# Joined stores and new instruction orders in a one-core vision transformer layer

## What is computed

```
p = img2patches(x)                                  # 1152 x 768
h = layernorm(layernorm(p) @ W + b)                 # patch embedding, 192 wide, in float32
h = h + attention(layernorm(h))                     # 12 heads of 16; cosine attention over the 32 images
                                                    #   at one patch position
h = h + bitlinear(silu(gate) * up)                  # up, gate = bitlinear(layernorm(h)); 192 -> 2 x 512 -> 192
```

## Time and profile before

| | |
|---|---|
| Median of three runs | 127.58 us |
| The profiled execution | 127.43 us, of which the span is 125.5 us |
| Busy, share of the span | PE 106.9 us (85%), DVE 102.5 (82%), ACT 86.1 (69%), POOL 70.9 (57%) |
| Chain that ended last, by engine | PE 33%, DVE 25%, POOL 18%, issue 9%, DMA 4%, ACT 3% |
| DMA | 7.77 MB; written 0.88 MB in 18 stores of 48 KB |

### The profile page before, as it was taken

How to read it: one execution, slowest core, us unless ns; L and a number is a source line. 1 busy time by engine, 2 the same in 40 slices (tenths; PEclk the granted TensorE clock), 3 DMA queues, 4 the chain that set the end, 5 groups by cost and what they waited for, 6 DMA issues and landing times.

```text
span 125.5 us, 4783 instructions
## 1 busy us (share of the span) xinstructions
PE 106.9 (85%) x1851; PEld 84.7 (67%) x1854; DVE 102.5 (82%) x384; ACT 86.1 (69%) x175; POOL 70.9 (57%) x164
## 2 busy tenths in 40 slices
PE   5998998999999998999999999899989976844500
PEld 5988898799787886976776766777567743423100
DVE  4039438999999999999999999999999999967200
ACT  0406537899998853296587995985999978996500
POOL 7002007349341096175269789998899898885000
PEclk9999999999999999999999999999999999999985
DMA  4999999969700000000000000000001010110110
GB/s 83 237 272 219 177 181 275 228 120 162 136 22 3 0 5 3 5 5 3 5 5 5 0 0 5 5 5 3 5 8 28 7 43 21 30 35 21 34 46 33
DMA packets 24095, 7.77 MB, mean 62 GB/s; under 512 B 20038, under 2 KB 23495, under 8 KB 24072
## 3 DMA queue, kind: packets, MB, share of 16 engines
q1 hardware_dynamic: 20838, 6.82, 27.0%
q10 hardware_dynamic: 3234, 0.64, 2.7%
HBM read 6.58 MB, written 0.88 MB: 59 GB/s over the span
## 4 chain that ended last, share of the span: by engine, by line
PE 33%; DVE 25%; POOL 18%; issue 9%; DMA 4%; ACT 3%; ACTq 2%; POOLq 0%; DVEq 0%
PE bank L662 7%; POOL yw L359 5%; DMA xs<-in_x_dram 4%; PE bank L667 3%; PE bank L684 3%; POOL r L367 3%; PE bank L685 3%; PE bank L646 3%; PE bank L713 2%; ACTq L242 2%; POOL yy L351 2%; DVE ss L913 2%; PE bank L701 2%; PE bank L584 2%; DVE mx L971 2%
## 5 line engine op out<-in xcount | busy, mean ns | idle before, releaser
L662 PE MATMUL bank<-w_emb_g,xT 128*128 128x192 f32 x72 | 13.5, 330 | 1.1 <-DVE h0s L879 1.0
L866 DVE BATCH_NORM_STATS2 bst<-xs 128x6 f32<-128x384 f32 x18 | 9.0, 540 | 6.0 <-DMA xs<-in_x_dram 6.0
L315 POOL TENSOR_TENSOR rs<-mv,mhalf 128x1 f32<-128x1 f32 x9 | 5.5, 609 | 14.6 <-DVE mv L888 14.6
L662 PEld LDWEIGHTS bank<-w_emb_g,xT 128*128 128x128 f32 x72 | 11.6, 190 | 2.2 <-issue 2.0
L461 ACT ACTIVATE xp<-xs,mv 128x768 f32<-128x768 f32 x9 | 8.4, 935 | 5.7 <-DVE mv L872 5.7
L577 PE MATMUL bank<-ident 128*128 128x128 f32 x60 | 8.8, 315 | 1.8 <-POOL ident L289 1.5
L359 POOL TENSOR_TENSOR yw<-yy,gout_bc 128x512 f32<-128x512 f32 x8 | 10.2, 1271 | 0.2
L311 POOL TENSOR_TENSOR rs<-mv,mhalf 128x1 f32<-128x1 f32 x9 | 5.2, 582 | 8.8 <-DVE mv L872 8.8
L713 PEld LDWEIGHTS bank<-vx,pT 32*32 32x32 f32 x864 | 8.2, 104 | 2.3 <-issue 2.3
L577 PEld LDWEIGHTS bank<-ident 128*128 128x128 f32 x60 | 8.3, 165 | 2.0 <-POOL ident L289 1.5
L713 PE MATMUL bank<-vx,pT 32*32 32x17 f32 x864 | 8.9, 180 | 0.2 <-issue 0.2
(11 more groups left out here) (158 smaller groups left out, 350.7 us busy)
## 6 DMA issues: line engine op xcount, KB each, us to landing
xs<-in_x_dram SPq DMA_DIRECT2D x30, 96.0 KB, 3.2
out_dram<-h_all SPq DMA_DIRECT2D x17, 48.0 KB
wi_raw<-in_L_ffn_w_in_dram SPq DMA_DIRECT2D x1, 768.0 KB, 7.5
xs<-in_x_dram ACTq DMA_DIRECT2D x6, 96.0 KB, 3.9
w_emb_sb<-in_L_tok_W_dram SPq DMA_DIRECT2D x1, 576.0 KB, 5.1
w_qkv_raw<-attn_in_proj_weight_dram SPq DMA_DIRECT2D x1, 432.0 KB
wo_raw<-in_L_ffn_w_out_dram SPq DMA_DIRECT2D x1, 384.0 KB, 8.1
gout_bc<-in_L_ffn_g_out_dram SPq DMA_DIRECT2D x1, 256.0 KB, 4.7
```

The lines of the kernel that those rows point to most:

```text
L662: nc.tensor.matmul(emb_bank, xT[:, t % 3, P * k:P * (k + 1)], w_emb_g[:, 3 * (k % 2) + k // 2, :], start=(k == 0), stop=False)
L866: nc.vector.bn_stats(bst1[:, t, 6 * n:6 * (n + 1)], pixels[:, 24 * n:24 * (n + 1), :]).then_inc(bst1_ok, 1)
```

## The change

Three things change.

1. `store` takes a number n of neighbouring tiles, and stores n x 192 contiguous numbers per row. SP now waits for tiles 0 to 2, then 3 to 5, then 6 and 7, then 8, so there are 8 stores where there were 18. ACT still issues the upper half of tile 8.
2. All four lists of orders (POOL, ACT, PE, DVE) are new. The steps in them are the same; none is added or left out.
3. Among the moves: `ry0_` of tiles 6 and later stand elsewhere against POOL's products, `yw_(8)` goes from ahead of `ax5_(7)` to behind `out_(5)`, `b1w` from behind `mv1_(0)` to the head of DVE's list, and on PE `qkvT` from ahead of `emb2(0)` to behind it.

```diff
-        def store(eng, t, half):
-
-            first = 2 * G * (t // WT) + t % WT + WT * half
-            eng.dma_start(out[:, first:first + G + 1:G, :].rearrange("b j d -> j b d"),
-                          h2_all[64 * half:64 * half + 64, t, :]).then_inc(stored, 16)
+        def store(eng, t, n, half):
+
+            pair, c = t // WT, t % WT
+            rows = out.rearrange("b (r h c) d -> h r b (c d)", r=G, h=2)
+            eng.dma_start(rows[half, 2 * pair:2 * pair + 2, :, D * c:D * (c + n)],
+                          h2_all[64 * half:64 * half + 64, t:t + n, :].rearrange("p t d -> p (t d)")).then_inc(stored, 16)
...
-            for t in range(T):
-                sp.wait_ge(out_ok, t + 1)
-                store(sp, t, 0)
-                if t < T - 1:
-                    store(sp, t, 1)
-            sp.wait_ge(stored, 16 * 2 * T)
+            for t, n in ((0, 3), (3, 3), (6, 2)):
+                sp.wait_ge(out_ok, t + n)
+                store(sp, t, n, 0)
+                store(sp, t, n, 1)
+            sp.wait_ge(out_ok, T)
+            store(sp, T - 1, 1, 0)
+            sp.wait_ge(stored, 16 * 8)
...
POOL, the stretch up to the first products of tile 4, and the end
-            kpad_(3); qn_(3); nm3_(6); s4_(0); e4_(0); rs2_(8); s4_(1); rs3_(7); e4_(1); f_h_(0); nm3_(7); kpad_(4); qn_(4)
-            c5_(0); f_h_(1); s4_(2); rs3_(8); e4_(2); kpad_(5); qn_(5); yy_(0); nm3_(8); c5_(1); f_h_(2); yw_(0); ms5_(0)
...
-            yw_(7); ms5_(7); c5_(8); r5_(7); s5_(7); f2_(5); ms5_(8); f2_(6); r5_(8); s5_(8); f2_(7); f2_(8)
+            qn_(3); nm3_(5); s4_(0); e4_(0); rs2_(8); rs3_(6); rs3_(7); nm3_(6); s4_(1); rs3_(8); nm3_(7); e4_(1); f_h_(0)
+            qn_(4); kpad_(4); f_h_(1); nm3_(8); s4_(2); c5_(0); c5_(1); kpad_(5); qn_(5); yy_(0); e4_(2); yw_(0); ms5_(0)
...
+            f2_(4); yw_(7); ms5_(7); c5_(8); r5_(7); s5_(7); f2_(5); ms5_(8); f2_(6); r5_(8); f2_(7); s5_(8); f2_(8)
...
PE, the start
-            warm(0); warm(1); xTa(0); bmm(); xTa(1, (xTl_ok, 1)); emb1(0, (p_bias, 1)); xTb(0); qkvT(); emb2(0)
-            xTa(2, (xTl_ok, 2)); xTb(1); emb1(1, (h0s_ok, 1)); emb2(1); xTb(2); emb1(2, (h0s_ok, 2)); xhT_(0, (xTh_ok, 3))
...
+            warm(0); warm(1); xTa(0); bmm(); xTb(0); xTa(1, (xTl_ok, 1)); emb1(0, (p_bias, 1)); xTb(1, (xTh_ok, 1)); emb2(0)
+            qkvT(); emb1(1, (h0s_ok, 1)); xTa(2); emb2(1); xTb(2); emb1(2, (h0s_ok, 2)); xhT_(0, (xTh_ok, 3)); emb2(2)
...
DVE, the start, the stretch with ry0_(6), and the end
-            bst1_(0); mv1_(0); b1w(); bst1_(1); mv1_(1); wg(); bst1_(2); bias(); mv1_(2); h0s_(0); bst2_(0); mv2_(0); hg_(0)
...
-            qT_(4); rb_(5); xc_(2); rv_(5); ss_(6); rn_(5); ssm_(6); ax4_(2); yg_(0); kT_(5); mx_(4); qT_(5); ry0_(6)
...
-            an5_(5); ax4_(8); ri5_(5); m4_(8); qs4_(8); qs5_(5); out_(3); yg_(7); ax5_(6); yy_(7); an5_(6); ri5_(6); out_(4)
-            qs5_(6); yg_(8); yy_(8); ax5_(7); yw_(8); an5_(7); ri5_(7); qs5_(7); out_(5); ax5_(8); out_(6); an5_(8); ri5_(8)
-            qs5_(8); out_(7); out_(8)
+            b1w(); bst1_(0); mv1_(0); bst1_(1); mv1_(1); wg(); lsm(); bst1_(2); mv1_(2); bias(); h0s_(0); bst2_(0); mv2_(0)
...
+            ry1_(5); ssm_(6); rb_(5); ry0_(6); rv_(5); ra_(6); rn_(5); yg_(0); rw_(6); mx_(4); rz_(6); kT_(5); qT_(5)
...
+            m4_(8); qs4_(8); an5_(5); yg_(7); out_(3); ri5_(5); qs5_(5); ax5_(6); yy_(7); an5_(6); ri5_(6); yg_(8); qs5_(6)
+            out_(4); yy_(8); ax5_(7); an5_(7); ri5_(7); qs5_(7); out_(5); yw_(8); ax5_(8); out_(6); an5_(8); ri5_(8)
+            qs5_(8); out_(7); out_(8)
```

More of the change, by code:

```diff
@@ L403, in _ @@
-            e4_(6); yy_(4); f2_(2); yw_(4); ms5_(4); f_h_(6); r5_(4); c5_(6); s5_(4); f2_(3); s4_(7); ms5_(5); e4_(7)
-            yw_(5); r5_(5); s4_(8); s5_(5); f_h_(7); e4_(8); ms5_(6); yw_(6); r5_(6); f_h_(8); s5_(6); f2_(4); c5_(7)
-            yw_(7); ms5_(7); c5_(8); r5_(7); s5_(7); f2_(5); ms5_(8); f2_(6); r5_(8); s5_(8); f2_(7); f2_(8)
+            rs1_(0); rs1_(1); rs2_(0); rs1_(2); rs3_(0); nm3_(0); rs2_(1); rs2_(2); rs1_(3); rs1_(4); rs3_(1); nm3_(1)
+            rs3_(2); rs2_(3); nm3_(2); rs2_(4); rs1_(5); rs3_(3); qn_(0); kpad_(0); nm3_(3); rs1_(6); rs2_(5); rs3_(4)
@@ new lines, in _ @@
+            qn_(1); kpad_(1); rs1_(7); gin(); rs2_(6); rs2_(7); kpad_(2); qn_(2); rs1_(8); rs3_(5); nm3_(4); kpad_(3)
+            qn_(3); nm3_(5); s4_(0); e4_(0); rs2_(8); rs3_(6); rs3_(7); nm3_(6); s4_(1); rs3_(8); nm3_(7); e4_(1); f_h_(0)
+            qn_(4); kpad_(4); f_h_(1); nm3_(8); s4_(2); c5_(0); c5_(1); kpad_(5); qn_(5); yy_(0); e4_(2); yw_(0); ms5_(0)
+            r5_(0); f_h_(2); s5_(0); kpad_(6); qn_(6); yy_(1); f2_(0); s4_(3); yw_(1); e4_(3); ms5_(1); c5_(2); yy_(2)
+            r5_(1); yw_(2); ms5_(2); s5_(1); s4_(4); f_h_(3); r5_(2); e4_(4); s5_(2); f2_(1); kpad_(7); f_h_(4); qn_(7)
@@ L407, in _ @@
+            s4_(5); c5_(3); e4_(5); f2_(2); qn_(8); kpad_(8); yy_(3); f_h_(5); c5_(4); yw_(3); ms5_(3); s4_(6); yy_(4)
+            e4_(6); yw_(4); c5_(5); r5_(3); ms5_(4); s5_(3); r5_(4); f_h_(6); s5_(4); f2_(3); s4_(7); c5_(6); ms5_(5)
+            e4_(7); r5_(5); yw_(5); f_h_(7); s5_(5); s4_(8); e4_(8); c5_(7); ms5_(6); yw_(6); r5_(6); f_h_(8); s5_(6)
+            f2_(4); yw_(7); ms5_(7); c5_(8); r5_(7); s5_(7); f2_(5); ms5_(8); f2_(6); r5_(8); f2_(7); s5_(8); f2_(8)
         @block.scalar
@@ new lines, in _ @@
+            emb1(4, (h0s_ok, 4)); xTb(5, (xTh_ok, 5)); emb2(4); woTp((p_qkvE, 3)); v_mm_(0); xhT_(1, (xTh_ok, 6)); wsum()
+            emb1(5, (h0s_ok, 5)); xhT_(2, (xhT_ok, 2)); qk_mm_(1, (qk_ok, 1)); emb2(5); v_mm_(1, (vx_ok, 1)); xTa(6)
+            sc(0, (p_oE, 1)); xhT_(3, (xhT_ok, 3)); qk_mm_(2, (qk_ok, 2)); emb1(6, (h0s_ok, 6)); xTb(6, (xhT_ok, 4))
+            v_mm_(2, (vx_ok, 2)); xTa(7); emb2(6); qk_mm_(3, (qk_ok, 3)); xTb(7); xTa(8, (xTl_ok, 8)); emb1(7, (h0s_ok, 7))
+            woT(); emb2(7); xTb(8); sc(1, (sm_ok, 1)); emb1(8, (h0s_ok, 8)); emb2(8); pv(0, (vx_ok, 3)); sc(2, (sm_ok, 2))
@@ L1082, in _ @@
-            ry0_(5); rn_(4); rsum_(3); bst4_(2); on_(3); ra_(5); kT_(4); rw_(5); m4_(1); rz_(5); mv4_(2); qs4_(1); ry1_(5)
-            qT_(4); rb_(5); xc_(2); rv_(5); ss_(6); rn_(5); ssm_(6); ax4_(2); yg_(0); kT_(5); mx_(4); qT_(5); ry0_(6)
-            sm_(4); ra_(6); rw_(6); m4_(2); rz_(6); qs4_(2); ry1_(6); yg_(1); mx_(5); pT_(4); rb_(6); rv_(6); sm_(5); rn_(6)
-            ax5_(0); ss_(7); kT_(6); h2_(3); an5_(0); bst4_(3); rsum_(4); mv4_(3); qT_(6); pT_(5); xc_(3); ssm_(7); ri5_(0)
-            ax4_(3); yg_(2); m4_(3); qs5_(0); on_(4); qs4_(3); mx_(6); ax5_(1); sm_(6); rsum_(5); ry0_(7); on_(5); ss_(8)
@@ L1087, in _ @@
-            pT_(6); h2_(4); ra_(7); ssm_(8); bst4_(4); rw_(7); mv4_(4); ry0_(8); xc_(4); h2_(5); rz_(7); bst4_(5); ax4_(4)
-            mv4_(5); rsum_(6); ry1_(7); ra_(8); m4_(4); on_(6); rb_(7); rw_(8); rv_(7); rz_(8); rn_(7); ry1_(8); qs4_(4)
-            ax5_(2); rb_(8); xc_(5); rv_(8); an5_(1); ax4_(5); kT_(7); rn_(8); qT_(7); m4_(5); yg_(3); qs4_(5); ri5_(1)
-            kT_(8); mx_(7); an5_(2); qs5_(1); sm_(7); ri5_(2); yg_(4); out_(0); h2_(6); qT_(8); bst4_(6); pT_(7); mv4_(6)
-            qs5_(2); ax5_(3); mx_(8); xc_(6); sm_(8); rsum_(7); on_(7); an5_(3); ax4_(6); ri5_(3); pT_(8); m4_(6); yg_(5)
@@ L1092, in _ @@
-            qs5_(3); qs4_(6); yy_(5); h2_(7); out_(1); bst4_(7); ax5_(4); rsum_(8); mv4_(7); on_(8); an5_(4); xc_(7)
-            out_(2); ax4_(7); ri5_(4); yg_(6); m4_(7); qs5_(4); qs4_(7); h2_(8); bst4_(8); mv4_(8); yy_(6); ax5_(5); xc_(8)
-            an5_(5); ax4_(8); ri5_(5); m4_(8); qs4_(8); qs5_(5); out_(3); yg_(7); ax5_(6); yy_(7); an5_(6); ri5_(6); out_(4)
-            qs5_(6); yg_(8); yy_(8); ax5_(7); yw_(8); an5_(7); ri5_(7); qs5_(7); out_(5); ax5_(8); out_(6); an5_(8); ri5_(8)
+            b1w(); bst1_(0); mv1_(0); bst1_(1); mv1_(1); wg(); lsm(); bst1_(2); mv1_(2); bias(); h0s_(0); bst2_(0); mv2_(0)
@@ new lines, in _ @@
+            hg_(0); h_(0); bst3_(0); mv3_(0); h0s_(1); bst1_(3); mv1_(3); bst2_(1); bst1_(4); mv2_(1); hg_(1); h0s_(2)
+            mv1_(4); bst1_(5); bst2_(2); h_(1); mv1_(5); mv2_(2); ss_(0); hg_(2); ssm_(0); h_(2); bst3_(1); ry0_(0); mv3_(1)
+            h0s_(3); bst3_(2); whs(); ra_(0); rw_(0); mv3_(2); bst2_(3); rz_(0); ry1_(0); mv2_(3); rb_(0); hg_(3); h0s_(4)
+            bst2_(4); rv_(0); mv2_(4); h_(3); hg_(4); bst3_(3); wmean_(); mv3_(3); h_(4); winv_(); rn_(0); bst1_(6); qT_(0)
+            mv1_(6); bst1_(7); kT_(0); h0s_(5); bst1_(8); mv1_(7); ss_(1); bst2_(5); bst3_(4); mv2_(5); mx_(0); mv3_(4)
@@ new lines, in _ @@
+            sm_(4); ax4_(2); ry1_(6); m4_(2); pT_(4); qs4_(2); mx_(5); rb_(6); ax5_(0); rv_(6); sm_(5); rn_(6); yg_(1)
+            an5_(0); kT_(6); h2_(3); ss_(7); bst4_(3); rsum_(4); ri5_(0); ssm_(7); mv4_(3); qT_(6); xc_(3); pT_(5); yg_(2)
+            on_(4); ax4_(3); ry0_(7); ss_(8); m4_(3); mx_(6); qs5_(0); qs4_(3); sm_(6); rsum_(5); ssm_(8); ax5_(1); on_(5)
```

(7 more changed lines are left out.)

99 lines of the change are left out of this document (42 added, 57 removed).

## The result

The changed kernel takes 130.76 us (median of four runs, 130.12 to 131.62); the kernel before took 127.78 beside it. The ratio is 1.026, with an interval of 1.022 to 1.030. It is slower, as forecast, but by 3.0 us of the medians (3.4 by the ratio) where the forecast was 1.6. The profiled execution took 131.24 us, with a span of 129.4.

The account below looks back on a forecast made before the run. A backlog in the two-engine store queue sets the end. Last byte at 112.6 + 13.6 = 126.2, plus 0.9 to the span's end, 127.1, plus 1.93 to the time: 129.0 us; range 126.9 to 130.8.

Parts of the forecast that it names:

- What bounds the kernel: At the end: a backlog in the store queue, on two of sixteen engines, beginning with tile 5; 257 KB left after 119 us.
- Part 1, the price of a store: Joined stores: bytes make the price, 89 to 97 ns per 2304-byte packet; 2.85 us for three tiles, 1.93 for two.
- Part 1, what is held back: Tiles 3 and 4 wait for tile 5, so 11.7 us of store service follow its `out_`, against 8.5 before.
- E5: End of `out_(5)` on DVE, from which the store tail is counted; 113.7 us before, forecast at 112.6.
- rival A: Packets count, not bytes, or joined stores use more engines: a joined store takes 1.06 us, time 124.4 us; 7%.
- I add 0.8 for slow stretches: Store queue after `out_(5)`: 0.8 us beyond full-rate service, scaled from the 1.3 lost before while new stores were issued.
- Part 2, E5 = 113.7 - 1.1 = 112.6: POOL's full stretch: moving `yw_(8)` saves 0.56 us and `rs3_(8)` 0.55, so `out_(5)` ends 1.1 us earlier.
- The start: Moves of `b1w` and `qkvT` at the first tiles: taken as 0, bounds -0.6 and +0.5 us.
- Tail: From the last stored byte to the end of the span: 0.9 us, as before.
- Rivals B and C: B: orders bring `out_(5)` to 111 us, time 127.4, 19%. C: orders worse by 1.5 us, time 130.5, 14%.
- the 117.5 to 118.5 given as a sign: End of `out_(8)` on DVE: expected at 117.5 to 118.5 us, earlier than before, while the time is longer.

Follow-up runs that it names:

- the last kernel: Only stores, the layer left out: one store of three tiles, two, four, then sixteen-engine groups; the first three took 4.1, 8.0 and 14.1 us.

## Why the forecast was right in sign and short in size

- **What bounds the kernel: right.** The backlog in the two-engine queue sets the end. With the same stores on sixteen engines the ratio falls from 1.026 to 0.964 in the new orders, and from 1.038 to 0.974 in the old ones.
- **Part 1, the price of a store: right at the full rate only.** 93 ns a packet; after 119 us the queue moves 49 GB/s, so 147 KB take 3.0 us at that rate and 2.85 at the 52 GB/s of the fast window. Over the whole queue nothing of the 1.0 us that the sum took off for joining is there (14.2 us joined, 14.1 single).
- **Part 1, what is held back: right.** 11.7 us of service stand behind E5 instead of 8.5. The kernel with single stores held back shows that this alone makes it slower, and rival A falls (share 0.13, not more engines, and 147 KB alone take 4.1 us, not 1.06).
- **The step that failed: "I add 0.8 for slow stretches (three groups instead of four arrive, so about 1.3 x 3/4, less a little)".** Stores run until about 128.7 us (61 KB are moved from 127.0 to 128.8), which is E5 + 15.3 with E5 at 113.38; the forecast was E5 + 13.6. The stores move from 114.5 us, 1.2 behind E5, to 128.7, and 11.7 is the service at the full rate, so the slow stretches are 14.2 - 11.7 = 2.5 us instead of 0.8. In the first 4 us 0.12 MB are moved where 51 GB/s would move 0.20: 1.6 us. The last 1.8 us run at 34 GB/s and cost some 0.5, and the 8.3 us between at 49 instead of 51 GB/s another 0.3. I had taken the slow rate of 115 to 119 us for a cost of arriving groups and scaled it down with their number. The stores-only kernels show that it comes with the stores themselves, with nothing else running. Had I scaled nothing, 1.3 would have stood there, and 129.5 as the time, still 1.2 us short: single stores lose 14.1 - 12.7 = 1.4 us against their own full rate, joined ones 2.5 against theirs, and that takes back what joining gains. An estimate from the queue before as a whole, 9.8 us for 8 stores, would have put 14.7 us on 12 of them and 131.2 on the time. For the profiled execution, 131.24 us, the errors add up: 1.7 us of slow stretches and 0.8 of E5, less 0.2 in the tail.
- **Part 2, E5 = 113.7 - 1.1 = 112.6: right, but for a wait that no term held.** In the profiled execution E5 is 113.4, and 0.74 of it is DVE's wait for images; in the two profiles of the new orders without that wait it is 112.3 and 112.6. The times of the three pairs of kernels agree (1.3 to 1.7 us). `r5_(7)` takes 0.57 instead of 1.13 us, and POOL's stretch from its first product behind the gap (65.52 us, below) to the end of `s5_(7)` (112.29) is 46.8 us instead of 112.63 - 64.98 = 47.7: 0.9 of the 1.1. This stretch starts 0.5 later than before, though, and in front of it `s4_(1)` waits 1.96 us for DVE. Its new place isn't the reason: in the new orders with single stores, where the images were in time, it waits 1.68 us as well, and the stretch starts at 64.47, 0.5 us earlier than before.
- **The start: counted as zero, and 0.4 was lost there.** PE's `emb1(1)` begins at 21.26, and at 20.88 before. It is inside my bounds; the 0.74 us of waiting for images that follow are not in them, and in the kernel before DVE had begun that step at 20.65 us without a wait.
- **Tail: 0.7 us** from the last byte to the end of the span, forecast 0.9. `out_(8)` ends at 118.58, at the edge of the 117.5 to 118.5 given as a sign.
- **Rivals B and C**, E5 at 111 or 1.5 us later, didn't come. The range, up to 130.8, just held the median of 130.76, and by luck: its upper end had been given to C's late orders, not to the store queue.

Timelines of POOL, after and then in the new orders with single stores, and the rows of line 929 (`ry0_`; min/median/max ns) and of PE's start:

```profile
63.15 0.78 POOL L333 TENSOR_TENSOR s<-mv,mhalf 128x1 f32<-128x1 f32 x1 [1.96 <-DVE mv L1003]
...
65.52 0.51 POOL L379 TENSOR_TENSOR qn<-qk,rn 128x192 f32<-128x192 f32 x1
```

```profile
62.06 0.78 POOL L331 TENSOR_TENSOR s<-mv,mhalf 128x1 f32<-128x1 f32 x1 [1.68 <-DVE mv L1001]
...
64.47 0.51 POOL L377 TENSOR_TENSOR qn<-qk,rn 128x192 f32<-128x192 f32 x1 [0.20 <-DVE rn L958]
```

```profile
L929 DVE TENSOR_SCALAR ry<-ssm x9: 139/170/305, 28.3 to 83.6; 128x24 int32<-128x24 int32 x9
```

```profile
21.26 1.54 PE L664 MATMUL bank<-w_emb_g,xT 128*128 128x192 f32 x8 [0.38 <-DVE h0s L881]
```

`ry0_(6)` takes 0.18 us, as forecast, and the longest `ry0_` falls from 522 to 305 ns. In the two stages from 65 us, DVE's idle time is 48.3 - 46.54 = 1.8 us as before: nothing was won from its gaps, and what the orders won stands in POOL's stretch.

The Trainium skill, "SBUF — State Buffer" (Who interferes with whom), had two instructions like `yw_` and `r5_` block each other, and by it `yw_(8)` should now have met `r5_(8)`. They overlap, 113.29 to 113.99 and 113.26 to 113.83, and take 0.70 and 0.57 us. In the kernel before, `r5_(7)` began 0.02 us ahead of `yw_(8)` and took 1.13, with 0.68 for `yw_(8)`. This repeats: in all three profiles with the old orders the lead is 17 to 21 ns and `r5_` takes 1.13 us, in all eight with the new ones it is 29 to 33 ns and `r5_` takes 0.57. So the trace of after doesn't agree with blocking in every such meeting. The outcome goes with some 10 ns of lead; that the lead decides it isn't shown.

## What to carry to other kernels

Before anything else about a store, read its share of the 16 engines: at 0.14, the share of about two, its bytes, not its packets, were a queue that set the end. Joining stores saved nothing there and delayed bytes, while changing the slowest dimension of the same store took the changed kernel from 2.6% above the kernel before to 3.6% below it. Where a queue has a backlog at the end, each transfer held back is added to it; and the price of a longer queue is best taken from a whole queue in the trace, slow start included, not from its fast middle with a correction.

## What the runs showed of the hardware

- Stores at the share of two engines start slowly: 29 to 36 GB/s in the first 3 to 4 us, then 44 to 51 (45 to 47 in packets of 768 bytes), with nothing else running as well as beside the layer. A whole queue of 590 KB takes 14.1 to 14.2 us, in packets of 768 or 2304 bytes.
- On sixteen engines 295 KB move at 151 GB/s (34.25 to 36.20 us of the last kernel), not at eight times the 50 of two engines.
- The end of `out_(5)` differs by 1.4 us between two executions with the same orders, 112.6 us in the kernel with a half issued later and 114.0 in the one on sixteen engines; DVE's wait for one image load, 0 and 1.04 us, makes most of it.
- A power of 128x1 on POOL beside a 128x512 product on DVE took 1.13 us when it began 17 to 21 ns ahead, and 0.57 at 29 to 33 ns.
